# Three of four token tiles ahead of the fourth through self attention, normalisation and gate logits, with products of constants at three waits of TensorE

## The reference

```python
x = x + _L0_xattn_ref(_layernorm(x), ctx_1024, mask, q_w, q_b, k_w, k_b, v_w, v_b)
x = x + _L0_attn_ref(_layernorm(x), W_q)
x = x + _L0_ffn_ref(_layernorm(x), gate_w, gate_b, w1, b1, w2, b2)

# _L0_xattn_ref: 16 heads of 32, softmax over 1601 context rows of which some are masked
# _L0_attn_ref: no softmax
q = einsum('bsh,oh->bso', hidden_states, W_q)
pre_attn = einsum('bso,bto->bst', q, hidden_states)
attention = einsum('bst,bth->bsh', pre_attn, hidden_states)
# _L0_ffn_ref: 8 experts of 2048 hidden units, each token goes to its best 2
logits = xf @ gate_w + gate_b
top_v, top_i = top_k(logits, 2); top_w = softmax(top_v)
out = out + cw[:, e:e + 1] * (relu(xf @ w1[e] + b1[e]) @ w2[e] + b2[e])
```

## Time and profile before

| | before |
|---|---|
| median of 3 runs | 1293.33 us (1292.92 to 1294.27) |
| the profiled execution: its own time | 1289.2 us |
| the profiled execution: span from first to last instruction | 1287.5 us |
| PE busy | 1246.4 us, 97% of the span |
| DVE busy | 842.4 us, 65% |
| ACT busy | 675.0 us, 52% |
| POOL busy | 159.2 us, 12% |
| mean granted clock of PE | 0.988 |

### The profile page before, as it was taken

The page is one execution under the profiler, slowest core; times in us unless marked ns, Lnnn a source line. Parts: engine busy times, 40 slices in busy tenths (PEclk is TensorE's granted clock), DMA queues, the critical chain, the costliest instruction groups (busy, mean ns, idle before and its releaser), DMA issues.

```text
span 1287.5 us, 22172 instructions
## 1 busy us (share of the span) xinstructions
PE 1246.4 (97%) x8497; PEld 1161.5 (90%) x8497; DVE 842.4 (65%) x2186; ACT 675.0 (52%) x1193; POOL 159.2 (12%) x86
## 2 busy tenths in 40 slices
PE   7999999999999999999999999999878999999997
PEld 6799999999999999999999999988767988989996
DVE  4556656566565666556566566685576788877877
ACT  5345545535544553464455455354444676767673
POOL 2203101300400220040031013000021000000012
PEclk9999999999999999999999999999969999999999
DMA  9002200310220040022022003100226667677763
GB/s 329 27 1 88 82 1 1 118 52 1 91 79 2 27 142 1 1 91 79 2 90 80 1 7 143 38 2 7 97 74 241 226 240 254 238 240 250 230 220 114
DMA packets 61506, 129.04 MB, mean 100 GB/s; under 512 B 3572, under 2 KB 21120, under 8 KB 61160
## 3 DMA queue, kind: packets, MB, share of 16 engines
q1 hardware_dynamic: 59240, 120.85, 27.4%
q0 software_dynamic: 2176, 6.95, 1.6%
HBM read 121.89 MB, written 15.34 MB: 107 GB/s over the span
## 4 chain that ended last, share of the span: by engine, by line
PE 92%; DVE 4%; ACT 2%; DMA 1%; issue 1%; POOL 0%; SPq 0%; POOLq 0%; DVEq 0%
PE ptp L830 24%; PE work L830 20%; PE work L1128 8%; PE pv L975 7%; PE ptp L959 7%; PE work L868 6%; PE work L1130 4%; PE ptp L1149 2%; PE ptp L1152 2%; PE ptp L1151 2%; PE ptp L1153 2%; PE ptp L1150 2%; PE work L837 2%; PE ptp L837 1%; DVE pt L1379 1%; DMA raw<-in_ctxT 1%
## 5 line engine op out<-in xcount | busy, mean ns | idle before, releaser
L830 PE MATMUL ptp<-vw_hi,cx_hi 128*128 128x256 f32 x832 | 241.8, 291 | 0.0
L830 PE MATMUL ptp<-vw_lo,cx_hi 128*128 128x256 f32 x832 | 235.4, 283 | 0.0
L830 PE MATMUL ptp<-vw_hi,cx_lo 128*128 128x256 f32 x832 | 235.4, 283 | 0.0
L518 POOL TENSOR_TENSOR cx_lo<-raw,cx_hi 128x1664 fp32r<-128x1664 f32 x30 | 113.8, 3792 | 666.3 <-ACT cx_hi L578 666.3
L830 PE MATMUL work<-cx_hi,kw_hi 128*128 128x400 f32 (+1 forms) x504 | 175.5, 348 | 2.9 <-POOL cx_lo L518 1.7
L830 PEld LDWEIGHTS ptp<-vw_hi,cx_hi 128*128 128x128 f32 x832 | 159.3, 191 | 17.0 <-issue 17.0
L830 PE MATMUL work<-cx_hi,kw_lo 128*128 128x400 f32 (+1 forms) x504 | 173.6, 345 | 0.0
L830 PE MATMUL work<-cx_lo,kw_hi 128*128 128x400 f32 (+1 forms) x504 | 173.2, 344 | 0.0
L1379 DVE TENSOR_TENSOR pt<-ptp,pt 128x512 fp32r<-128x512 f32 (+1 forms) x224 | 141.3, 650 | 33.3 <-ACT pt L578 29.8
L830 PEld LDWEIGHTS ptp<-vw_lo,cx_hi 128*128 128x128 f32 x832 | 159.3, 191 | 0.0
L830 PEld LDWEIGHTS ptp<-vw_hi,cx_lo 128*128 128x128 f32 x832 | 159.3, 191 | 0.0
(11 more groups left out here) (268 smaller groups left out, 2384.9 us busy)
## 6 DMA issues: line engine op xcount, KB each, us to landing
w1raw<-in_w SPq DMA_DIRECT2D x32, 1024.0 KB, 5.1
w2raw<-in_w SPq DMA_DIRECT2D x32, 1024.0 KB, 6.9
raw<-in_ctxT SPq DMA_DIRECT2D x31, 832.0 KB, 6.3
pr<-in_mask SPq DMA_DIRECT2D x8, 800.5 KB, 4.4
xrow<-x_rows SPq DMA_DIRECT2D x7, 256.0 KB, 6.2
y_rows<-y_out_rows POOLq DMA_DIRECT2D x7, 256.0 KB, 2.4
xin<-in_x SPq DMA_DIRECT2D x1, 1024.0 KB, 8.9
qwraw<-in_qwT SPq DMA_DIRECT2D x1, 1024.0 KB, 11.1
```

Of the source, the lines that this page charges most:

```text
L518: pool.tensor_tensor(cx[1][:, :, sl], raw[:, k % 2], cx[0][:, :, sl].bitcast(F32), ALU.subtract).then_inc(c_lo, 1)
L830: last = pe.matmul(dst, lhs(i, c), rhs(j, c), start=(c == 0 and (i, j) == (0, 0)), stop=(c == n - 1 and (i, j) == (1, 0)))
```

## The change

1. **Late attention.** In the last batch the step "t" stands ahead of "q": PE transposes the first probabilities of group 2 before it makes the query block. DVE's `row_weights` of tile 3 goes from the end of group 2 to the step "q", and `group_out` of group 2 goes behind the subtractions of group 3. ACT's `fold` of group 3 gets a wait on `pv_free`, and DVE's `group_out` of group 3 one on `att_rows`.
2. **Self block.** Tiles 0 to 2 go first: their scores, values, residual, norm (`layer_norm` number 4), transposes and logits. Tile 3's query block, scores, values, norm (number 5), transpose and logits come behind on PE, and behind the norm of the others on DVE. Banks of `turn_banks` change. ACT copies the first piece of w1 ahead of the query copies, and the first piece of w2 and the second of w1 ahead of the roots; the high halves of tiles 0 to 2 (`tokens_hi`) stand ahead of their transposed copies.
3. **First expert.** On DVE the low half of the first w2 piece goes from the norm to just ahead of the experts, that of the second w2 piece from ahead of the gather to the expert's second piece, and the block that copies `placeT` and `cwT` and works out the output rows goes from ahead of the experts to behind the first piece's hidden rows (`places_and_weights`).
4. **Constants.** `keep_busy(bank, n)` lets PE multiply `ident` by `ones` n times, ahead of the first keys (12), ahead of the wait for the choice (12) and ahead of the wait for the masks and low halves (8). The results are not used.

```diff
-            steps += v[6:] + e[2:] + turned + queried + t + w[:1] + w[1:]
+            steps += v[6:] + e[2:] + turned + t + queried + w
...
-        turn_banks = [yb[2], work[2], yb[0], yb[1]]
+        turn_banks = [work[1], work[2], yb[2], work[3]]
...
                 act.wait_ge(pt_used, NPT * b + TPH * (g + 1) + PTD)
+                if last and g == 3:
+                    act.wait_ge(pv_free, 4 * b + g + 1)
...
+            def keep_busy(bank, n):
+
+                for _ in range(n):
+                    pe.matmul(bank[:, 0:P], ident[:], ones[:], start=True, stop=True)
...
+            keep_busy(work[3], 12)
             READY = {(0, 0): ((kw0_hi, w_hi), (c0_hi, c_hi)), (0, 1): ((c0_lo, c_lo),), (1, 0): ((kw0_lo, w_lo),)}
...
-            for t in range(TT):
-                last = logits(t)
-            last.then_inc(m_full, 1)
+            for t in range(EARLY):
+                logits(t)
+            pe.wait_ge(ln2, TT + EARLY + 1)
+            turn_tile(EARLY, turn_banks[EARLY]).then_inc(m_full, 1)
+            logits(EARLY).then_inc(m_full, 1)
+            keep_busy(yb[3], 12)
             pe.wait_ge(zeroed, 7)
             pe.wait_ge(chosen_done, 1)
...
+            keep_busy(yb[3], 8)
             pe.wait_ge(x_lo, TT)
...
-                    if kind == "w":
-                        if last and a == 2:
-                            row_weights(range(EARLY, TT))
+                    if kind == "w" and not (last and a == 2):
+                        if last and a == 3:
+                            group_out(b, last, 2)
+                            dve.wait_ge(att_rows, 4 * b + 3)
                         group_out(b, last, a)
...
+            w1_part(0, 0)
             dve.wait_ge(zeroed, 7)
             for t in range(EARLY):
                 blocks(t, work[t])
-            w1_part(0, 0)
             add(0, yb[0])
+            add(1, yb[3])
+            add(2, yb[2])
+            layer_norm(xs, hn, ln2, 4, range(EARLY))
             blocks(EARLY, yb[1])
-            add(1, yb[3])
-            add(3, work[1])
-            add(2, work[0])
-            layer_norm(xs, hn, ln2, 4)
-            w2_part(0, 0)
+            add(EARLY, yb[1])
+            layer_norm(xs, hn, ln2, 5, range(EARLY, TT))
...
-                    if not (fresh and p < 2):
+                    if not (fresh and p == 0):
                         w2_part(n, p)
...
             w1_part(0, 1)
-            w2_part(0, 1)
...
-            dve.wait_ge(m_full, filled("places"))
...
+            w2_part(0, 0)
             experts(0)
```

More of the change, by code:

```diff
@@ L96 @@
 TPH = KT // 2 + 1
-FILLED = (["q0_1", "att3", "b1", "q0_2", "q0_3", "pre0", "pre1", "turn0_3", "pre2", "q1", "own0", "pre3", "own1", "own3",
-           "own2", "turn1_0", "turn1_1", "turn1_2", "turn1_3", "logits", "earlier", "total", "places", "weights",
+FILLED = (["q0_1", "att3", "b1", "q0_2", "q0_3", "turn0_3", "pre0", "pre1", "pre2", "own0", "own1", "own2", "q1", "pre3",
+           "own3", "turn1_0", "turn1_1", "turn1_2", "turn1_3", "logits", "earlier", "total", "places", "weights",
            "b2_0", "b2_1", "b2_2", "b2_3"])
@@ L707, in w2_part @@
                 copy(w2s[0][:, s], w2raw[:, s], w2_hi)
-            def first_weights(p):
-                w1_part(0, 0, p, True)
-                w2_part(0, 0, p, True)
             def turned(k, t, bank):
@@ L721, in early_query, with tokens_hi @@
                 copy(gT[:, m_, MINE], work[m_ - 1][:, MINE], m_out)
+            def tokens_hi(t):
+                act.wait_ge(ln2, TT + t + 1)
+                copy(xn[0][:, t], hn[:, t], x_hi)
+            act.wait_ge(att_over, 4)
+            w1_part(0, 0, 0, True)
             early_query(1)
@@ L728, in _ @@
                 early_query(m_)
-            act.wait_ge(att_over, 4)
             turned(0, EARLY, yb[1])
-            w1_part(0, 0, 0, True)
+            w2_part(0, 0, 0, True)
+            w1_part(0, 0, 1, True)
+            root(4, range(EARLY))
             act.wait_ge(m_full, filled("q1"))
-            copy(gT[:, :, EARLY * P:T], yb[2][:].rearrange("p (c n) -> p c n", c=C), m_out)
-            w2_part(0, 0, 0, True)
-            root(4, range(TT))
-            for t in range(TT):
+            copy(gT[:, :, EARLY * P:T], work[3][:].rearrange("p (c n) -> p c n", c=C), m_out)
+            for t in range(EARLY):
+                tokens_hi(t)
+            for t in range(EARLY):
+                if t == EARLY - 1:
+                    root(5, range(EARLY, TT))
                 turned(1, t, turn_banks[t])
-            for t in range(TT):
-                act.wait_ge(ln2, TT + t + 1)
-                copy(xn[0][:, t], hn[:, t], x_hi)
-            first_weights(1)
+            turned(1, EARLY, turn_banks[EARLY])
+            tokens_hi(EARLY)
+            w2_part(0, 0, 1, True)
             def gathered(n):
@@ L1413, in body @@
                         layer_norm(xs, hn, ln2, 2, range(EARLY))
+                    if kind == "q":
+                        row_weights(range(EARLY, TT))
                     if kind in "vskanq":
@@ L1609, in expert @@
                     if p == 0 and isinstance(n, int) and n == 0:
+                        places_and_weights()
                         biases()
```

57 lines of the change are left out of this document (29 added, 28 removed).

## The result

| | before | after |
|---|---|---|
| median (4 runs each, same chip) | 1293.12 us (1292.24 to 1294.27) | 1277.32 us (1277.12 to 1278.78) |
| the profiled execution: own time, span | 1289.2, 1287.5 us | 1278.78, 1277.1 us |
| mean granted clock | 0.988 | 0.993 |

The ratio is 0.9881, with a 95% interval from 0.9868 to 0.9895: 15.8 us faster. I had forecast 1281.0 us, 12.3 us less; the result lies in the range, at its fast side. The two profiled executions are only 10.4 us apart. That of before was 4 us faster than before's median, that of after 1.5 us slower than its own. Where the medians gain more than the profiles is the question of the experiments.

What follows compares the result with a forecast made beforehand. PE bounds the kernel (92% of the span), so edits pay at its waits or low clock. 13.9 us at the first hidden rows plus 2.2, less 3.3 for clock and 0.5 for ports, gave 12.3: 1281.0 us, range 1276.5 to 1286.5.

Steps and rivals of the forecast that it cites:

- Query behind the transposes: End of attention: 8 of 12 transposes move into PE's 2.30 us wait, so weighting starts 1.5 us earlier.
- Row weights and the sums of group 2: End of attention: PE's 2.32 us wait shrinks to about 0.5, saving 1.8 us, plus 1.1 us of clock.
- Self block: Tiles 0 to 2 first: logits at 943.2 instead of 955.2, 12.0 us in all so far at full clock.
- Choice: 12 constant products against PE's 2.42 us wait for the choice: cost 0.2 us at full clock, 2.7 at half.
- Gather: The gather's 32 rows took 5.7 us, 18 of them at half clock; at full clock 3.6, so 2.1 saved.
- Clock, -3.3: Clock falls between tile 3's values and the constants and returns within the constants, costing 3.3 us; forecast's chance 48%.
- Ports, -0.5: POOL's low halves against DVE's small steps of tile 3's norm, sharing SBUF ports: 0.5 us lost.
- First expert, 2.2: PE's 2.20 us wait for DVE's sums in expert 0 goes, saving 2.2 us.
- First keys, 0: Constants at the start speed the first keys, but the 2 us are lost again as a wait: 0.
- the holding clock: Rival, 22%: short bursts on tile 3 keep the clock up, so 3.3 us loss falls away: 1277.7 us.
- The start's fall: Rival, 17%: clock low at 23.59 us after the early keys, slowing the next 24 rows by 2 to 4 us: 1284.0.
- the queue in expert 0: Rival, 7%: DVE and ACT work queues up, PE waits up to 1.5 us at each piece of expert 0: 1286.0.

Runs made afterwards that it cites:

- before_again: The kernel before, run once more with no edit: 1294.15 us (12 runs); its profiled execution took 1294.83 us.
- constants_alone: The kernel before with the three sets of constant products and none of the moves: 1295.27 us, ratio 1.0011.
- old_late_attention: The changed kernel without constants, with the order at the end of attention put back as before: 1282.29 us, ratio 0.9914.
- old_self_block: The kernel before with the late attention and first expert changed, no constants, so only the self block is old: 1281.86 us, ratio 0.9910.
- spread_biases: The changed kernel without constants, its four bias products spread between blocks of the second hidden piece: 1278.47 us, ratio 0.9879.
- the moves alone: The changed kernel with all three sets of constant products left out: 1275.54 us, ratio 0.9863 to the kernel before.
- full_rows: The changed kernel without constants, its bias products padded from 8 to 128 rows, 120 of them zero: 1275.87 us, ratio 0.9872.

## Why the prediction was right, and where it was off

Counted from the transposed tiles (895.59 and 896.49), as the prediction's chain goes:

- **Query behind the transposes**: 1.5 us forecast, 1.67 measured (8.44 to 6.77). Right.
- **Row weights and the sums of group 2**: the wait of 2.32 us became two of 0.23 and 0.25, forecast 0.5; the fall of the clock beside it went. Tile 3's attention came 4.3 us earlier in the profiles (4.0 forecast). By medians the part is worth 6.8 us. Mis-sized: the term counted one short fall, 1.1 us. The other two profiles of the old order on the kernel before have a second one, in the query (4.24 us in before_again, 4.51 in constants_alone, in place of 2.82); that of old_late_attention has only the one.
- **Self block**: first add at 928.54, 927.64 without the late start (927.85 forecast); tile 3's norm ended at 941.35, 940.45 without the late start (940.7). Logits at 944.89 against 955.29, 11.3 us after the correction; 12.0 at full clock, less the eight rows at half. Right. Taken back alone the part was worth 6.3 us by medians and not 8.0 (old_self_block).
- **Choice**: constants at 0.21 a row, 2.4 us late: my half clock case, 2.7. **Masks**: 0.3 at full clock, forecast 0.5. **Gather**: right.
- **Clock, -3.3**: it fell near 942.6 and rose near 949.5; eight rows of logits lost 0.8 us, the constants 2.5. The size is right, and so is "between tile 3's values and the constants". The first hidden rows came 10.5 us earlier where 13.9 less 3.3 is 10.6.
- **Ports, -0.5**: not seen, and not tested. POOL made three low halves from 935.97 in 3.76 us, 1.25 each, as in the earlier trace rows. DVE's three tiles of `hn` (1.46 us from 934.68) were nearly done by then and overlap with them by 0.17 us; what DVE did beside POOL were copies (0.47 for two) and an addition (0.69) that read a PSUM bank, and statistics of one tile (0.69), at the durations that they have in before. No operation of DVE with two large SBUF inputs ran beside POOL there. So nothing here bears on the exclusive lock that the Trainium skill states (SBUF — State Buffer, on the shared port pair).
- **First expert, 2.2**: the term that was most mis-sized. The wait of 2.20 us went, as said. But in after's profile the clock fell earlier than before and lasted longer, so that the second product piece came 15.6 us behind the first hidden row, against 17.1, and PE's last row came 1.2 us earlier by this part and not 2.2. The ten microseconds from the first bias product on, in before and in after:

```profile
979.00:989.00 10.00, 9.17 (x27) 5.74 (x26) 7.54 (x17) 2.78 (x7) 0.00 (x0) 0.83 0.76 263
```

```profile
967.00:977.00 10.00, 9.17 (x21) 5.08 (x21) 7.34 (x8) 0.00 (x0) 0.00 (x0) 0.66 0.78 264
```

  That is 3.4 us of half clock against 6.8; the prediction put the clock in the first expert at nothing. In the medians the miss is the other way: 2.20 us was the shortest such wait, the other profiles that have DVE's block there and do not delay POOL's DMAs show 4.05, 3.25 and 4.13 us, with half clock behind, and taking the part back cost 8.6 us.
- **First keys, 0**: right, shown by the wait of 1.60 us that appears with the constants and goes without.

The recorded sum at the first hidden rows holds an error: 12.0 - 0.2 - 0.5 + 2.1 is 13.4 and not 13.9, and no run shows the half microsecond called rounding. Without it the forecast is 11.8 us, where the two profiled executions gave 11.7 from the transposed tiles to PE's last row.

The forecast was 3.7 us too slow mainly in how it was carried to the median. I made the sum against one profiled execution and carried it to the median as it stood. That execution was the fastest of this kernel on record (the next took 1291.3), with 0.988 of clock where the median one has 0.987, and with a short wait where three other profiles have a long one. The moves removed places where executions differ, so the median gains what the lucky execution never lost. Before_again against after bears it out, as one pair of profiles: from the transposed tiles to PE's last row 390.5 us against 373.6, 16.8 us, where the first profile gives 11.7. Of the 5.2 us between the two profiles of before, 1.7 had come up by the first hidden rows, by the clock, and 1.85 are the longer wait.

Of the rivals, the holding clock named 1277.7, near the result, but for a reason that did not happen: the clock did fall. The start's fall and the queue in expert 0 did not show. The constants stood in the sum with costs and gains at four places; that they lose in total follows from those terms (2.1 - 0.2 - 0.5 of gain against 2.5 of the 3.3 us of clock) and was not drawn. The medians bear it out at 1.8 us, not clear of noise.

## What to carry to other kernels

Three moves gave the time, each of work that stood ahead of what PE waited for: at the end of attention, in the self block and ahead of the first expert. Filling the waits did not. A filling must be sized at the lower clock, with its rows' duration there against the shortest wait, or it becomes the wait. And a wait found in one profile is one draw: run the kernel before several times with the clock of each run, and price a removed wait by the typical execution.

## What the runs showed that I had not expected

- The clock can fall while PE is busy without a gap: after 11 us of it without a wait, then 11 us at 0.53, among products with 8 rows and hidden products (spread_biases). With the bias products padded to 128 rows, at the same duration (six rows in 2.84 us in the moves alone and 2.76 in full_rows), the clock of the stretch was 1.00 in both profiles of it.
- Two DVE copies from the PSUM banks began up to 2.0 us after the transposes they wait for had ended, in three of four profiles in which POOL had its indirect DMAs of 0.96 us to issue at about that time; with the DMAs later they began within 0.1 us. Why is open.
- At the start the granted clock reads 1.00 from the first microsecond, while 24 rows of constants took 5.10 us, 0.21 each, the duration of half clock elsewhere. The column can't be trusted there; the rows' durations can.
